# Three small operations of a router moved from VectorE to ScalarE, and three left out

## The reference, cut to what matters

```
logits = h @ gate_w.T
scores = sqrt(softplus(logits))
_, topk_idx = top_k(scores + bias, 6)
topk_w = take_along_axis(scores, topk_idx); topk_w = topk_w / sum(topk_w) * 1.5
onehot = one_hot(topk_idx.reshape(-1), 32)
pos = cumsum(onehot) - 1            # place of a token in the queue of its expert, 192 places
...                                  # the experts' matmuls on the placed rows
```

## Time and profile before

| what | us |
|---|---|
| median of three runs (lowest, highest) | 3671.74 (3670.55, 3674.1) |
| the profiled execution's own time | 3667.42 |
| its span in the profile | 3665.6 |
| busy: TensorE | 3231.0 (88%) |
| busy: VectorE | 2201.1 (60%) |
| busy: GpSimd | 1757.7 (48%) |
| busy: ScalarE | 1204.0 (33%) |
| mean granted TensorE clock | 0.934 of full |

### The profile page before, as it was taken

The page is one execution under the profiler, slowest core; times in us unless marked ns, Lnnn a source line. Parts: engine busy times, 40 slices in busy tenths (PEclk is TensorE's granted clock), DMA queues, the critical chain, the costliest instruction groups (busy, mean ns, idle before and its releaser), DMA issues. The chain is left out here.

```text
span 3665.6 us, 61864 instructions
## 1 busy us (share of the span) xinstructions
PE 3231.0 (88%) x20358; PEld 1668.7 (46%) x20366; DVE 2201.1 (60%) x5978; ACT 1204.0 (33%) x2733; POOL 1757.7 (48%) x988
## 2 busy tenths in 40 slices
PE   4567999999998999989998999989999998687998
PEld 2334444444444444444444444444444444255775
DVE  6843444566646664666466746674667567755564
ACT  3661333233333332333333323332333233311111
POOL 5640454455545554555455535553555355643222
PEclk8878999999999999999999999999999998888999
DMA  5762200011111001100100010101010100205996
GB/s 186 298 257 74 84 30 18 30 75 55 54 65 50 18 22 47 35 13 16 53 22 29 13 56 16 36 13 53 18 35 13 53 18 12 71 5 161 257 257 149
DMA packets 121804, 253.60 MB, mean 69 GB/s; under 512 B 38748, under 2 KB 39388, under 8 KB 118928
## 3 DMA queue, kind: packets, MB, share of 16 engines
q1 hardware_dynamic: 77152, 200.36, 16.2%
q0 software_dynamic: 44048, 49.26, 5.2%
q10 hardware_dynamic: 288, 0.00, 0.0%
HBM read 144.61 MB, written 202.16 MB: 95 GB/s over the span
## 5 line engine op out<-in xcount | busy, mean ns | idle before, releaser
L966 POOL TENSOR_TENSOR a_first_probs<-a_first_probs,a_probs 128x2048 f32<-128x2048 f32 (+3 forms) x320 | 1030.4, 3220 | 1044.4 <-ACT a_probs L1046 956.1
L1192 DVE CUSTOM_DVE_ANT_0 a_unused<-a_ps_ring,a_work 128x512 bf16<-128x512 f32 (+3 forms) x1536 | 778.3, 554 | 843.1 <-PE a_ps_ring L1541 838.8
L1046 ACT ACTIVATE a_probs<-a_ps_ring 128x512 f32<-128x512 f32 (+3 forms) x1280 | 508.8, 473 | 472.4 <-PE a_ps_ring L1575 297.8
L1565 PE MATMUL a_ps_ring<-a_k_t,a_q_t 32*128 32x512 f32 (+3 forms) x3072 | 440.2, 543 | 112.8 <-DVE a_row_max L1192 89.7
L1541 PE MATMUL a_ps_ring<-a_q_t,a_k_t 32*128 32x512 f32 (+3 forms) x3072 | 390.9, 550 | 14.4 <-DVE a_row_max L1192 12.5
L977 POOL DMA_INDIRECT d_slots<-a_rows,a_place_i x349 | 355.1, 1018 | 70.8 <-issue 62.4
L1565 PEld LDWEIGHTS a_ps_ring<-a_k_t,a_q_t 32*128 32x128 f32 x3072 | 158.9, 188 | 314.0 <-DVE a_row_max L1192 137.5
L1541 PEld LDWEIGHTS a_ps_ring<-a_q_t,a_k_t 32*128 32x128 f32 x3072 | 144.0, 191 | 285.7 <-issue 259.8
L1588 PE MATMUL a_ps_heads<-a_probs,a_values 128*32 128x512 f32 (+3 forms) x2560 | 269.1, 494 | 0.0
L973 POOL TENSOR_TENSOR a_attn_t<-a_attn_t,a_sum_inv 128x512 f32<-128x512 f32 x64 | 84.9, 1327 | 380.4 <-DVE a_sum_inv L1207 380.3
L1046 ACT ACTIVATE a_first_probs<-a_ps_ring 128x512 f32<-128x512 f32 x256 | 135.7, 604 | 373.6 <-PE a_ps_ring L1575 348.6
(11 more groups left out here) (289 smaller groups left out, 4430.5 us busy)
## 6 DMA issues: line engine op xcount, KB each, us to landing
d_hidden<-e_hidden SPq DMA_DIRECT2D x8, 2048.0 KB, 8.8
d_normed_t<-e_normed_t SPq DMA_DIRECT2D x8, 2048.0 KB, 11.8
a_work<-d_normed_t SPq DMA_DIRECT2D x7, 2048.0 KB, 7.9
a_hidden<-d_hidden SPq DMA_DIRECT2D x56, 256.0 KB, 2.7
out<-a_hidden SPq DMA_DIRECT2D x56, 256.0 KB
d_slots<-a_rows SPq DMA_DIRECT2D x32, 408.8 KB, 5.5
x_rows<-d_slots SPq DMA_DIRECT2D x32, 408.8 KB
x_w_gate<-w_gate SPq DMA_DIRECT2D x16, 512.0 KB, 6.4
```

What stands on the lines that cost most here:

```text
L966: nc.gpsimd.tensor_tensor(total_of, total_of, probs_of(m)[:, :, 0:width], ALU.add).then_inc(added, 1)
L1046: nc.scalar.activation(probs_of(m)[:, h, 0:width], score_bank(m, h)[:, 0:width], ACT.Exp).then_inc(exp_done, 1)
L1192: nc.vector.tensor_tensor_reduce(unused[:, (HG * k + h) % N_UNUSED, 0:width], row_bank(k, h)[:, 0:width], decay[:, at:at + width], 1.0, NE ...
L1565: nc.tensor.matmul(score_bank(m, h)[:, 0:width], q_t[st.g][dims, j * P:(j + 1) * P], k_t[st.g][dims, i0:i0 + width], start=True, stop=False)
```

## The change

ScalarE gets a `soft_parts` of its own, at the same place in its order (group 5, last gap): |x| and max(x, 0), straight from the logits' bank, which the second frees. Its exponential now takes exp(-1 x |x|), and a third instruction of `soft_plus` forms w = 1 + e. VectorE loses `soft_parts` (three instructions) and the sum 1 + e. In `count_chosen` it reads the uint32 indices as they are in the comparison, and the reduction writes bf16 directly, with max in place of add; both casts go. `find_places` reads `top_at` and `chosen_b` in place of `top_f` and `soft_ln`. The buffers stay as they were.

```
-            def soft_parts(k, use, chain):
-                logits = use.bank[:, 0:k.n * E].rearrange("p (j e) -> p j e", j=k.n)
-                dve.wait_ge(use.full, use.n + 1)
-                chain.done(nc.vector.tensor_scalar(k.plus, logits, 0.0, None, ALU.max))
-                nc.vector.tensor_scalar(k.minus_abs, logits, 0.0, None, ALU.min).then_inc(use.free, 1)
-                chain.wait()
-                dve.wait_ge(use.free, use.n + 1)
-                nc.vector.tensor_tensor(k.minus_abs, k.minus_abs, k.plus, ALU.subtract).then_inc(minus_abs_done, 1)
+            def soft_parts(k, use):
+                logits = use.bank[:, 0:k.n * E].rearrange("p (j e) -> p j e", j=k.n)
+                act.wait_ge(use.full, use.n + 1)
+                nc.scalar.activation(k.size, logits, ACT.Abs).then_inc(abs_done, 1)
+                nc.scalar.activation(k.plus, logits, ACT.Relu).then_inc(use.free, 1)
...
             def soft_plus(x, k=here):
-                act.wait_ge(minus_abs_done, x + 1)
-                nc.scalar.activation(k.minus_abs, k.minus_abs, ACT.Exp).then_inc(soft_e_done, 1)
+                act.wait_ge(abs_done, x + 1)
+                nc.scalar.activation(k.size, k.size, ACT.Exp, scale=-1.0).then_inc(soft_e_done, 1)
                 act.wait_ge(soft_e_done, x + 1)
-                nc.scalar.activation(k.soft_ln, k.minus_abs, ACT.Ln, bias=1.0).then_inc(soft_ln_done, 1)
+                nc.scalar.activation(k.soft_w, k.size, ACT.Identity, bias=1.0).then_inc(soft_w_done, 1)
+                nc.scalar.activation(k.soft_ln, k.size, ACT.Ln, bias=1.0).then_inc(soft_ln_done, 1)
...
-            def soft_sum(x, k, chain):
-                dve.wait_ge(soft_e_done, x + 1)
-                chain.done(nc.vector.tensor_scalar(k.soft_w, k.minus_abs, 1.0, None, ALU.add))
-                chain.wait()
+            def soft_sum(x, k, use, chain):
+                dve.wait_ge(soft_w_done, x + 1)
...
+                dve.wait_ge(use.free, use.n + 1)
                 nc.vector.scalar_tensor_tensor(k.soft, k.soft, SOFT_LEAST, k.plus, ALU.max, ALU.add).then_inc(soft_done, 1)
...
             def count_chosen(k, chain):
                 chain.wait()
-                chain.done(nc.vector.tensor_copy(k.top_f, k.top_at))
-                chain.wait()
                 chain.done(nc.vector.tensor_tensor(
                     k.is_top, experts_row[:].unsqueeze(1).unsqueeze(1).broadcast_to((P, k.n, TOPK, E)),
-                    k.top_f[:, :, 0:TOPK].unsqueeze(3).broadcast_to((P, k.n, TOPK, E)), ALU.is_equal))
-                chain.wait()
-                chain.done(nc.vector.tensor_reduce(k.soft_ln, k.is_top.rearrange("p j k e -> p j e k"), AXX, ALU.add))
-                chain.wait()
-                nc.vector.tensor_copy(k.chosen_b, k.soft_ln).then_inc(counted, 1)
+                    k.top_at[:, :, 0:TOPK].unsqueeze(3).broadcast_to((P, k.n, TOPK, E)), ALU.is_equal))
+                chain.wait()
+                nc.vector.tensor_reduce(k.chosen_b, k.is_top.rearrange("p j k e -> p j e k"), AXX, ALU.max).then_inc(counted, 1)
```

More of the change, by code:

```diff
@@ L1116, in take_dense @@
                         take_turned(rows_t, arg, use)
+                    elif kind == "route":
+                        soft_parts(here, use)
                     elif kind == "up":
@@ L1155, in _ @@
             take_turned(late_rows_t[0], 1, late("turn", 1))
+            soft_parts(late_parts[0], late("route", 0))
             soft_plus(LATE_X + 0, late_parts[0])
@@ L1164, in _ @@
             soften_gate(LATE_X + 0, 1, late_inner[0], late_gate_up[0][1], late("up", 1, 0))
+            soft_parts(late_parts[1], late("route", 1))
             soft_plus(LATE_X + 1, late_parts[1])
@@ L1309, in find_places @@
                                         ALU.mult).then_inc(use.free, 1)
-                chain.done(nc.vector.tensor_tensor(k.soft_ln, k.soft_ln, k.score, ALU.mult))
+                chain.done(nc.vector.tensor_tensor(k.soft_ln, k.chosen_b, k.score, ALU.mult))
                 chain.wait()
@@ L1345, in find_late_places @@
                 chain.done(nc.vector.reciprocal(k.total_inv, k.total))
[L1346 removed]
+                chain.done(nc.vector.scalar_tensor_tensor(k.place, k.top_at[:, :, 0:TOPK], float(CAP), k.place,
                                                           ALU.mult, ALU.add))
@@ L1386, in take_dense @@
                         add_residual(st.t, arg, use)
-                    elif kind == "route":
-                        soft_parts(here, use, chain)
                     elif kind == "place":
@@ L1403, in tail_events @@
                 if (m, after) == SOFT_SUM_AT[first]:
-                    soft_sum(x, here, chain)
+                    soft_sum(x, here, dense(st.number("route", 0)), chain)
                 if (m, after) == GATE_AT[first][0]:
@@ L1481, in _ @@
             add_late(6, late("out", 6))
-            soft_parts(late_parts[0], late("route", 0), chain)
             late_stats(6, chain)
-            soft_sum(LATE_X + 0, late_parts[0], chain)
+            soft_sum(LATE_X + 0, late_parts[0], late("route", 0), chain)
             add_late(7, late("out", 7))
@@ L1492, in _ @@
             late_gate(0, 0, chain)
-            soft_parts(late_parts[1], late("route", 1), chain)
-            soft_sum(LATE_X + 1, late_parts[1], chain)
+            soft_sum(LATE_X + 1, late_parts[1], late("route", 1), chain)
             late_gate(0, 1, chain)
```

22 lines of the change are left out of this document (11 added, 11 removed).

## The result

The kernel after takes 3626.47 us in the median (3623.76 to 3632.62, 4 runs), the kernel before, on the same chip, 3671.14 (3669.16 to 3674.1, 4 runs). The ratio is 0.9877, 95% interval 0.9862 to 0.9893: 44.7 us less. Forecast was 3628.0 us, 44 less. The profiled execution took 3624.72 us with a span of 3622.9, against 3667.42 and 3665.6: 42.7 less. The time is right; several of the steps behind it are not, as the experiments and the traces show.

A forecast was written before the change was run, and what follows sets the result against it. TensorE, busy 88% of the span, was taken as the bound, with waits for VectorE's row maxima and L1308. Terms 37.4 + 3 + 3 + 1 = 44 us took the 3671.74 us median to 3628, range 3600 to 3648.

The forecast's parts named there:

- The cast as the cause, 37.4 us: Marks' cast L1301 on VectorE waits for GpSimd's port and delays the row maxima; removal saves 1.87 us in 20 steps.
- the 1.7 us of room: On VectorE, between the reduction's end by 1266.0 and 1267.71, when the maxima could start; delays within it cost nothing.
- The cast of the indices (L1293) goes ... I count 0.: On VectorE before the comparison: its 1.08 us move into comparison L1295, which ends where it ends now; gain 0.
- It stays, and the gain passes through it: TensorE's wait at L1640 for L1308: both ends move forward together, so it stays near 80 us in 28 waits.
- The clock, 3 us.: TensorE's 1.2 GHz stretch shrinks to the g = 0 steps' shape: 0.46 us in a third of 20 steps; bounds 0, 34.
- The last step, 3 us.: TensorE waits 8.65 us for L1301; three removed instructions stand in VectorE's chain; 3 us gained, bounds 0 and 8.65.
- The tail, 1 us: GpSimd's 12.27 us wait for the second half's places: two casts fewer and earlier softplus gain 1 us, bounds 0 and 4.
- ScalarE's additions and `soft_parts`, 0.: Groups 5 and 6: Abs and Relu fit ScalarE's idle time, VectorE's removed work is not waited for; 0, at worst 24 us.
- The clock did not stay up: Rival: TensorE's clock no longer falls at L1640, 34 us come on top, 3594 us; chance 0.10.
- The port did not take it back: Rival: VectorE's gate meets GpSimd's instructions instead, 16 us given back and 4 more lost, 3648 us; chance 0.12.
- No effect: Rival: the bf16 reduction itself needs the port and is as long as L1301, 3668 to 3672 us; chance 0.04.
- slower: Rival: behind group 11's waits TensorE's half-rate stretch lasts into the next step's projections, 3702 us; chance 0.04.

The follow-up runs named there:

- e2: The kernel after with the cast of the marks to bf16 put back: ratio 0.9897 to the kernel before, 38 us less.
- e4: The kernel before with only the index cast (L1293) left out, uint32 read directly: ratio 0.991, 34 us less.
- e12: The kernel before with the last two of group 10's four exponentials done in 64-column pieces on ScalarE in steps with g > 0: ratio 0.9905, 36 us less.
- e1: The kernel before with only the marks' cast (L1301) removed, the reduction writing bf16: ratio 0.9906, 35 us less.
- e3: The kernel before with only the softplus parts moved to ScalarE, both casts kept: ratio 0.9976, 9 us less.
- e6: The kernel before with GpSimd's L973 moved from group 10 to group 11: ratio 0.9968, 12 us less.
- e11: The kernel after with the second gate's reciprocal moved ahead of group 10's row maxima: ratio 0.9791 to the kernel before, 3595.39 us.
- e5: The kernel before with the marks' cast replaced by a second reduction writing bf16: ratio 0.9888, 40 us less.
- e9: The kernel before with a small two-column reduction added between the reduction L1299 and the marks' cast: ratio 1.0011.

## Why the prediction was right, and where it was not

*The cast as the cause, 37.4 us.* Right in size: the waits for the maxima fell by 37.1 us, by 1.87 us in the step shown. Not right is the statement that it "stands still until GpSimd has left the memory port that both engines need", if it is read as the cast's own cost: GpSimd's L973 alone makes it 1.35 us, which lies in the 1.7 us of room and costs nothing. The 1.87 us came from its standing for a second instruction as well. The Trainium skill (SBUF — State Buffer, section "SBUF: two separate sides") speaks of a lock for a whole instruction; e2, e4 and e12 agree (1.35 us beside 1.31 of L973), and before shows what happens when the next one is ready in time.

*"The cast of the indices (L1293) goes ... I count 0."* This failed, and it is the largest step that did. The step said that the 1.08 us "move into L1295, which would end where it ends now". They do not go over in full. The same place before and in e4:

```profile
1264.66 1.34 POOL L977 DMA_INDIRECT d_slots<-a_rows,a_place_i  x1 [0.15 <-issue]
1265.17 0.80 DVE L1299 TENSOR_REDUCE a_soft_ln<-a_is_top 128x64 f32<-128x384 bf16 x1
```

```profile
1252.18 1.46 DVE L1293 TENSOR_TENSOR a_is_top<-a_experts_row,a_late_top_at 128x384 bf16<-128x384 f32 x1
1253.38 1.13 POOL L977 DMA_INDIRECT d_slots<-a_rows,a_place_i  x1 [0.16 <-issue]
1253.67 0.82 DVE L1297 TENSOR_REDUCE a_soft_ln<-a_is_top 128x64 f32<-128x384 bf16 x1
```

From the start of the first of these VectorE instructions (L1293, the cast in the earlier trace rows, the comparison in e4) to the reduction's start it is 1.71 us before and 1.49 in e4. By this 0.2 us the reduction came earlier against ScalarE's exponentials. L973 came earlier with it: it follows L977, which ends within 0.03 us of the reduction in both. That was enough for the cast to slip in: 34 us for this edit alone. That the timing against the exponentials is what counts, e12 shows; that the reduction holds L977, and so L973, is only what the lines look like. In the sum the failed step stays hidden, since with the marks' cast gone nothing is left to rescue: e1, without this edit, has maxima's waits of 52.8 us, the kernel after 52.6. So at the maxima the two casts' gains are alternatives, not terms of a sum.

*"It stays, and the gain passes through it"* (L1640's wait, "still near 80 us"). The gain did pass through: from L1565's restart behind the maxima to the start of L1640 (L1559 and L1634 after), the 20 steps with g > 0 take 103.5 us in all before and 101.9 after. The size of the wait was wrong, 97.9 us: TensorE does its work between the two waits at the 2.4 GHz level now, and waits out at the second what it saves there. The 17.0 us more of this wait are matched by its busy time, which fell by 9.4 us in all, though in the first 690 us of the profile, the embedding, it rose from 528.7 to 535.3: 16 us less in what follows.

*The clock, 3 us.* Near in size, wrong in shape. From the start of L1640 to that of the next L1541 the same 20 steps take 2.2 us less in all. But the steps with g = 0, which I took as the pattern, changed too: behind their L1640 the stretch at 1.2 GHz was 3.4 us long in four of seven before, and is 6.8 us long in six of seven now. From the L1640 of a step with g = 3 to that of the next step, with g = 0, the kernel after takes 6.1 us more in six such pairs. Why is open.

From the first of these L1640 to the last, the profile after has 39.2 us less: 36.9 by the maxima's waits, against the forecast's 37.4, and 2.3 by all the rest.

*The last step, 3 us.* From the L1640 before it to its own it takes 0.4 us less, 68.7 in place of 69.1. TensorE's wait for the marks there is 8.1 us in place of 8.65. *The tail, 1 us:* from L1640 of the last step (3201.6 before, 3162.3 after) to the end of the span the kernel after has 3.4 us less. GpSimd's wait of 12.27 us is 10.70 now:

```profile
3264.49 0.98 POOL L978 DMA_INDIRECT d_slots<-a_work,a_late_place_i  x1 [10.70 <-DVE a_late_place_i L1356]
```

So the forecast had 3 and 1 for these two, and 0.4 and 3.4 were measured. That the sum of the two came out is luck.

*ScalarE's additions and `soft_parts`, 0.* The cover was there, as forecast: group 6's exponentials wait for TensorE as before. But e3 says that this part alone is worth 9 us on its chip, where the steps counted 0 and the last step and the tail 4 in all. The savings of e1 and e3 make 44 together, the whole of the change. Where e3's 9 us lie is open. The Trainium skill (ScalarE: Activation LUTs, section "Rules for kernel authors") advises VectorE for relu, max and add; here the move to ScalarE made the kernel 0.24% faster (e3), so the measurement decides against it for this place.

*The rivals.* The clock did not stay up: in the step shown it is at the 1.2 GHz level for 6.7 us in place of 10.2. The port did not take it back in this change (the comparison keeps the wait it inherited, the reduction has none), but it did in e6, and about half of the gain in e11. No effect and slower fell with the result.

So the largest term was right in mechanism and size (37.4 forecast, 36.9 measured), and its condition was missing: that GpSimd's next instruction is ready in time. That the rest came out as well, 7 forecast and 5.8 measured in the span, is partly luck: two of its terms are off by 2 to 3 us each and set each other off, and the 9 us of e3 had no place in the steps.

## What to carry to other kernels

A small VectorE instruction of a kind that waits for GpSimd can cost all that GpSimd runs without a gap from there, so look at whether GpSimd's next instruction is ready when the present one ends. In e4 a shift of 0.2 us against ScalarE's exponentials decided 34 us, in e12 one of 0.4 us decided 36. Before you add up the gains of several edits at one wait, ask whether each alone would remove it: a chain that is late by a race is mended by any one of them. When a wait has gone, look for the next on the same chain and split what stands behind it: instructions that no GpSimd work holds up (the reciprocal here) into idle time ahead, the others away from GpSimd's.

## What the runs showed of the hardware that I had not expected

- A waiting VectorE cast went in between two GpSimd instructions where the second became ready 0.13 us or less before the first ended, or later, and stood for both where it was ready 0.26 us or more ahead: 1.35 against 3.65 us. No step lies between. In e12 this was set by ScalarE alone.
- The reduction (bf16 in, 128x384) takes 0.79 to 0.83 us and the reciprocal (128x256) 1.74 to 1.76 us with or without GpSimd work beside them (before, after, e5, e11). The casts, the comparison with uint32 (0.49 and 1.46 us), the gate's first product (0.42 and 0.96) and the clamp (0.49 and 1.85) are longer beside it.
- GpSimd's indirect DMA instruction, 1.00 us elsewhere, takes 1.34 us beside the comparison and the reduction of before (the line of L977 above) and 1.13 in e4, and ends within 0.03 us of the end of VectorE's reduction in before, e4 and e9. That the reduction holds it up is what this looks like; it wasn't tried.
- Comparing uint32 with f32 costs no more than f32 with f32: 0.49 us at least against 0.56 in the kernel before.
- Cutting two exponentials of 128x256 into four of 128x64 each (e12) made the last of them end 0.4 us later: 1.35 us behind L973's start in place of 0.97.
